# Turning the attention stream over the loop's boundary, own task orders outside the loop, and two PSUM banks kept for the rotary tiles

## The chip, the core and the metric

The kernel runs on one core of one Trainium2 chip. The metric is the device time of one execution in microseconds; the time before is the median of three executions. One execution was also taken by the hardware profiler, and every row shown below is from it.

## The reference

The input is 16 sequences of 512 tokens with 128 features. Each sequence goes through a parameter-free layer norm, and the normed sequence feeds two independent branches, whose results are added to the input:

```python
# branch 1: causal attention, 16 heads of 64
qkv = x @ W_qkv + b_qkv                       # 128 -> 3072
scores = einsum(Q, K) / 8 + causal mask (-10000)
vals = softmax(scores) @ V
branch1 = vals @ W_out + b_out                # 1024 -> 128

# branch 2: two layers of a local transformer, 8 heads of 64, window 64
h = shift_token(x); q, k, v = split(h @ wqkv)     # 128 -> 1536
q, k = l2norm(q) * qs, l2norm(k) * ks
q, k = rotary_xpos(q, k)
o = softmax over own and previous window of 64, masked to distance <= 64
x = x + o @ wo
h = layernorm(shift_token(x)); a, g = split(h @ w1 + b1)
x = x + (a * gelu(g)) @ w2 + b2
```

## The kernel before, in words

Everything works on one sequence at a time, as 4 tiles of 128 tokens. The five engines run one program each, and they all go through the same list of 167 named tasks, `SCHEDULE`; each engine does its own share of each task, in list order. Semaphores link them. A task's name is its kind, the layer where there are two, and the tile or head pair: `("a_max", 3)`, `("f_qk", 1, 2)`.

Attention (`a_...`) takes its 16 heads as 8 pairs. For a pair, PE makes Q and K (`a_proj`, three fp32r products each, since the weights and x are split in a high and a low part), every second pair also V (`a_v`), then scores in bf16 for the row maximum (`a_max`: six PSUM banks, read by VectorE, DVE, at L875), transposes the negated maxima (`a_neg`), makes the transposed fp32 scores with the maxima and the masks added in (`a_st`: six banks, read by ScalarE's exponential at L733), multiplies with V (`a_pv`, once a head), transposes the result (`a_ot`), and adds its share of the output projection into a bank of its own (`a_out`). `a_end` takes that bank out.

The local transformer (`f_...`) of a layer has `f_qk` and `f_v` for each of 4 tiles, then `f_qkt` (transposes of the turned q and k), then 4 head pairs with `f_max`, `f_neg`, `f_st`, `f_pv` and `f_ot`, then `f_wo`, and a serial tail: `f_mean`, `f_var`, `f_rep`, `f_gate`, three `f_up`, `f_down`. In `f_qk`, PE fills two banks (q and k); ScalarE squares each, and DVE reads each four times for the rotary products (L930, L932, L933) and sums the squares (L935), which frees the bank. GpSimd takes the power -1/2 (L662) and scales. `f_wo` ends in DVE's residual addition at L948, once in each layer. `out` closes the sequence.

PSUM has 8 banks. Bank 7 is the output accumulator. The other seven are a ring: each use in the list takes the next bank, whatever it is for, and PE waits in `claim` until the last use of that bank has been read. Since PE goes through the list in order, one slow reader holds up all that comes behind.

The order of the list is made when the program is written out, by `by_ready_time`. It merges three streams greedily: layer 0 of the next sequence with the norm, layer 1 of the current sequence with `out`, and the eight pairs of attention of the current sequence with the transposition `xt` of the next one. Each step takes the stream whose head could start first by a table of costs (`STEPS`), with `f_qk` tasks at least 15 and `a_proj` tasks 20 units apart.

So each pass of the hardware loop does attention and layer 1 of sequence i, and norm, `xt` and layer 0 of sequence i + 1. There are 16 passes. Ahead of them, `before_first` does the tasks that `ahead` names (norm, `xt`, layer 0) for the first sequence, with nothing beside them, and raises the semaphores for those left out. Before that, the setup loads all parameters from the SyncE queue, makes the constants on GpSimd, turns the rotary tables with the scales (L818), and splits W_qkv in six pieces through `yT`, one load, one ScalarE copy (L685) and one DVE subtraction (L824) at a time. The norm of the first sequence comes behind the last subtraction. In the code these are at L559 to L569 (SyncE), L683 to L686 (ScalarE), L813 to L829 (DVE), L1004 to L1007 and L1249 to L1254 (TensorE, PE).

Of the kernel before, what the change touches and what calls it, by code (L numbers as in the profile page):

```python
# [15 lines left out]
P = 128  # L16
# [36 lines left out]
RING = 7  # L53

# [53 lines left out]
ROTARY, PAIR = 15.0, 20.0
# [14 lines left out]
def needs(task):  # L123

    kind, at = task[0], task[1:]
    if kind in ("a_max", "a_st"):
        return [(("a_neg", *at), 9) if kind == "a_st" else (("a_proj", *at), 1)]
# [28 lines left out]
def by_ready_time(streams):  # L156


    free = {"pe": 0.0, "act": 0.0, "dve": 0.0, "pool": 0.0}
    slots, used = [0.0] * RING, 0  # L160
    done, out, n = {}, [], [0] * len(streams)
    rotated = -ROTARY

    def ready(task):
        at = max([done[t][min(k, len(done[t]) - 1)] for t, k in needs(task)], default=0.0)
        if task[0] == "a_proj":
            at = max(at, PAIR * task[1])
        if task[0] == "f_qk":
            at = max(at, rotated + ROTARY)
        for k in range(min(BANKS.get(task[0], 0), 4)):  # L170
            at = max(at, slots[(used + k) % RING])
        return at

    while any(k < len(part) for k, part in zip(n, streams)):
        heads = [(max(ready(part[k]), free["pe"]), side) for side, (k, part) in enumerate(zip(n, streams))
                 if k < len(part) and all(t in done for t, _ in needs(part[k]))]
# [3 lines left out]
        rotated = start if task[0] == "f_qk" else rotated  # L180
# [5 lines left out]
        for k, (engine, us, lead) in enumerate(steps):  # L186
# [3 lines left out]
            if k + 1 == reads:  # L190
                count = BANKS[task[0]]
                for b in range(count):
                    slots[(used + b) % RING] = begun + us * (b + 1) / count
        used += BANKS.get(task[0], 0)
# [4 lines left out]

SCHEDULE = by_ready_time([[("norm",)] + heavy_tasks(0) + tail_tasks(0),  # L200
                          heavy_tasks(1) + tail_tasks(1) + [("out",)],
                          attention_tasks() + [("xt",)]])


def ahead(task):

    return task[0] in ("norm", "xt", "f_first") or (task[0][:2] == "f_" and len(task) > 1 and task[1] == 0)
# [8 lines left out]
assert in_order(("norm",), ("f_first",), ("xt",)) and in_order(("a_proj", PAIRS - 1), ("xt",))  # L216
assert in_order(("a_v", PAIRS // 2 - 1, 1), ("xt",)) and in_order(("a_end",), ("out",))


def earlier(task, which):  # L220


    at = SCHEDULE.index(task)
    for k in range(at - 1, at - 1 - len(SCHEDULE), -1):
        if which(SCHEDULE[k]):
            return SCHEDULE[k], k < 0
    raise ValueError(task)


class Signal:  # L230
# [1055 lines left out]
```

## Time and profile before

| | us |
|---|---|
| three timed executions | 3816.88, 3819.74, 3820.7 |
| median | 3819.74 |
| profiled execution | 3820.81 |
| its span, first to last instruction | 3819.0 |
| PE busy | 3265.4 |
| DVE busy | 2102.0 |
| ScalarE (ACT) busy | 1694.3 |
| GpSimd (POOL) busy | 985.5 |

The busy times are unions of the instructions' durations on an engine. The granted clock, PEclk, is the share of full speed that PE was given, on average over a stretch. "Idle before" is time in which an engine had nothing running, with the instruction that released it. L12 is line 12 of the kernel file.

### The profile page before, as it was taken

The page shows a single profiled execution, that of the slowest core. Times are in us where ns is not written, and L with a number is a line of the kernel's source. Part 1 is how long each engine was busy: PE and PEld are TensorE (multiplying, and loading weights), DVE is VectorE, ACT ScalarE, POOL GpSimd, SP SyncE. Part 2 cuts the span into 40 slices and gives each one's busy share as a digit, 9 for nine tenths or more (in the row PEclk, how much of TensorE's full clock was granted, in tenths as well). Part 3 has the DMA queues.
Part 4 walks back from the last instruction along what each step waited for, and adds up shares of the span by engine and source line. Part 5 has one row for each costly group of instructions (what it writes and reads, how often), then busy time and mean ns, then how long its engine had stood idle before and what let it go on. Part 6 is the DMA issues. An engine that isn't in the chain of part 4 may idle for free.

```text
span 3819.0 us, 95524 instructions
## 1 busy us (share of the span) xinstructions
PE 3265.4 (86%) x35044; PEld 2173.1 (57%) x35044; DVE 2102.0 (55%) x7233; ACT 1694.3 (44%) x3181; POOL 985.5 (26%) x753
## 2 busy tenths in 40 slices
PE   1689898897989889898898989889898988979898
PEld 0356565564656556465565656556565655646565
DVE  2265464646556465564646556464655646465464
ACT  1245354544535445453444535444453535445353
POOL 2132230413224041331303223040322304132140
PEclk9799999999999999999999999999999999999999
DMA  3000000000000000000000000000000000000000
GB/s 79 1 7 2 10 2 10 2 2 10 2 10 2 5 7 2 10 2 10 2 2 10 2 10 2 10 2 2 10 2 10 2 11 2 2 7 2 7 2 4
DMA packets 42468, 26.45 MB, mean 7 GB/s; under 512 B 13107, under 2 KB 40669, under 8 KB 41949
## 3 DMA queue, kind: packets, MB, share of 16 engines
q1 hardware_dynamic: 41948, 19.56, 1.8%
q8 instruction: 323, 5.29, 0.6%
q14 instruction: 197, 1.61, 0.1%
HBM read 14.96 MB, written 4.19 MB: 5 GB/s over the span
## 4 chain that ended last, share of the span: by engine, by line
issue 41%; PE 32%; DVE 16%; ACT 6%; POOL 3%; SPq 1%; DMA 0%; DVEq 0%; ACTq 0%; POOLq 0%; PEldq 0%
PE bank L1103 4%; PE bank L1147 4%; DVE ss L935 3%; PE bank L1190 3%; DVE scratch L930 3%; PE bank L1021 2%; PE bank L1133 2%; DVE scratch L932 2%; PE bank L1205 2%; DVE scratch L933 2%; ACT scratch L767 2%; DVE scratch L943 2%; ACT probs L733 2%; PE bank L1125 2%; PE bank L1175 1%
## 5 line engine op out<-in xcount | busy, mean ns | idle before, releaser
L662 POOL TENSOR_TENSOR rnorm<-ssc,minus_half 128x8 f32<-128x8 f32 x264 | 484.4, 1835 | 991.5 <-DVE ssc L937 988.9
L875 DVE CUSTOM_DVE_ANT_0 bank<-bank,future 128x128 f32<-128x128 f32 (+3 forms) x1024 | 467.3, 529 | 142.1 <-PE bank L1065 140.1
L890 DVE CUSTOM_DVE_ANT_0 bank<-bank,band 128x192 f32<-128x192 f32 x1056 | 341.5, 397 | 281.2 <-PE bank L1084 275.7
L1103 PE MATMUL bank<-Qa,Ka 64*128 64x512 f32 (+3 forms) x2048 | 391.1, 464 | 50.2 <-DVE ss L935 36.1
L733 ACT ACTIVATE probs<-bank 128x512 f32<-128x512 f32 (+1 forms) x768 | 347.0, 530 | 195.8 <-PE bank L1112 195.6
L1147 PEld LDWEIGHTS bank<-Va,probs 128*64 128x64 f32 x10240 | 336.6, 143 | 116.9 <-issue 106.8
L767 ACT ACTIVATE scratch<-bank 128x512 f32<-128x512 f32 x264 | 158.7, 601 | 509.9 <-DVE ss L935 286.3
L1147 PE MATMUL bank<-Va,probs 128*64 128x65 f32 x10240 | 373.1, 230 | 0.7
L651 POOL TENSOR_TENSOR lrstd<-lvar,minus_half 128x4 f32<-128x4 f32 x33 | 33.4, 1012 | 1303.2 <-DVE lvar L953 1303.2
L741 ACT ACTIVATE lprobs<-bank 128x384 f32<-128x384 f32 x528 | 226.8, 491 | 205.1 <-PE bank L1135 202.0
L1190 PE MATMUL bank<-Lqkv,resid 128*128 128x512 f32 x528 | 283.3, 662 | 32.4 <-ACT resid L756 23.4
L930 DVE TENSOR_TENSOR scratch<-bank,rope_t 128x512 f32<-128x512 f32 x264 | 182.6, 692 | 190.3 <-ACT scratch L767 183.9
L1159 PE MATMUL bank<-Vf,lprobs 128*64 128x65 f32 x2112 | 236.9, 227 | 27.1 <-DVE ss L935 16.3
L1133 PE MATMUL bank<-Qf,Kf 64*128 64x192 f32 (+1 forms) x2112 | 241.1, 326 | 0.0
L1159 PEld LDWEIGHTS bank<-Vf,lprobs 128*64 128x64 f32 x2112 | 185.7, 138 | 71.2 <-issue 50.3
L1160 PE MATMUL bank<-Vf,lprobs 128*64 128x65 f32 x2112 | 221.1, 240 | 0.0
L1133 PEld LDWEIGHTS bank<-Qf,Kf 64*128 64x128 f32 x2112 | 182.9, 195 | 34.7
L1103 PEld LDWEIGHTS bank<-Qa,Ka 64*128 64x128 f32 x2048 | 157.8, 187 | 78.0 <-DVE ss L935 46.3
L690 ACT ACTIVATE Qf<-bank 128x512 f32<-128x512 f32 x264 | 160.4, 608 | 85.3 <-PE bank L1021 83.0
L1163 PE MATMUL bank<-Vf,lprobs 128*64 128x65 f32 x1584 | 198.1, 223 | 0.0
L1125 PE MATMUL bank<-outside,row_of 64*128 64x384 bf16 x1056 | 136.3, 336 | 70.1 <-ACT negfT L725 40.1
L690 ACT ACTIVATE Qa<-bank,bqkv 128x512 f32<-128x512 f32 x128 | 89.1, 696 | 239.3 <-PE bank L1016 239.3
(150 smaller groups left out, 7112.1 us busy)
## 6 DMA issues: line engine op xcount, KB each, us to landing
x_res<-in_L_attn_x SPq DMA_DIRECT2D x16, 256.0 KB, 2.9
x_rows<-in_L_attn_x SPq DMA_DIRECT2D x16, 256.0 KB, 3.1
out<-yT SPq DMA_DIRECT2D x16, 256.0 KB, 2.7
Lqkv<-in_L_ffn_wqkv SPq DMA_DIRECT2D x2, 768.0 KB
yT<-in_L_attn_W_qkv SPq DMA_DIRECT2D x6, 256.0 KB, 2.7
rope_t<-in_rope SPq DMA_DIRECT2D x8, 128.0 KB
Lw<-in_L_ffn_w SPq DMA_DIRECT2D x2, 341.0 KB
Lwo<-in_L_ffn_wo SPq DMA_DIRECT2D x2, 256.0 KB
```

The lines of the kernel that those rows point to most:

```text
L662: g.tensor_tensor(rnorm[s][:, :], ssc[s][:, :], minus_half[:, :], ALU.pow).then_inc(rnorm_ready.sem, 1)
L690: psum.raise_read(a.activation(dst, src, func, **kw), task, mark)
L733: psum.raise_read(a.activation(probs[j][:, at:at + n], psum.bank(task, (u, j))[:, 0:n], ACT.Exp, scale=float(HEAD) ** -0.5), task, (u, j))
L767: a.activation(squares, psum.bank(task, c)[:, :], ACT.Square).then_inc(squares_ready.sem, 1)
L875: ins = v.tensor_tensor_reduce(psum.bank(task, (u, j))[:, at:at + n], psum.bank(task, (u, j))[:, at:at + n], future[:, SEQ - n:SEQ], 1.0, ...
L890: ins = v.tensor_tensor_reduce(psum.bank(task, (u, j))[:, k * BAND:(k + 1) * BAND], psum.bank(task, (u, j))[:, k * BAND:(k + 1) * BAND], b ...
L930: v.tensor_tensor(heads(turn_a), src, table(0, 0, HEAD), ALU.mult)
L1103: mm(bank[j][:, at:end], Ka[p % 2][HALF[j], tile(k)], Qa[p % 2][HALF[j], queries], start=True, stop=False)
L1133: mm(bank[j][:, at:at + n], Kf[l][HALF[j], p, tile(t)], Qf[l][HALF[j], p, queries], start=False, stop=False)
L1147: ins = mm(bank[part, t * (HEAD + 1):(t + 1) * (HEAD + 1)], probs[j][:, at + part.start:at + part.stop], Va[p // 2 % 2][:, k, 2 * (p % 2) ...
L1159: mm(bank[HALF[0], to], lprobs[j][:, t, HALF[0]], Vf[l][:, t, 2 * p + j, :], start=True, stop=(t == 0))
L1190: psum.raise_filled(mm(bank[:, :], resid[l][:, tile(t)], Lqkv[l][:, c * INNER:(c + 1) * INNER], start=True, stop=True), task, m)
```

## The change

1. The attention stream is turned by four pairs. `A_BEGUN` is the rounds of pairs up to the middle, `A_REST` the others and `a_end`. A pass now does, in the third stream, `A_REST` of sequence i, then `xt` and `A_BEGUN` of sequence i + 1. `ahead` names `A_BEGUN` too.
2. The loop makes 15 passes. Ahead of it stands the list `FIRST` (norm, layer 0, `xt`, `A_BEGUN` of the first sequence), behind it the list `LAST` (layer 1, `out`, `A_REST` of the last), each ordered by the planner for itself, with 11 and 20 units between `f_qk` and `a_proj`. In the loop they are 15 and 24. `earlier`, `Signal` and `Ring` learn which of the three lists a use is in.
3. The seven banks become two rings: five banks for all uses but `f_qk`, two for `f_qk` alone. `claims` waits for both banks of a pair before the first product.
4. The setup is reordered. SyncE loads x, Lqkv of layer 0, its tables and scales, then W_qkv in two halves into space of layer 1's Q and K tiles, then the rest. GpSimd makes six constants, does its share of the first norm, and makes the rest. The split of W_qkv stands inside `xt` of the first sequence; turned tables of layer 0 stand inside its first `f_qk`, and waits for weights, masks and parameters stand at the first task that needs them.

```diff
 RING = 7
+TURNED, LONG = ("f_qk",), 2
...
+A_BEGUN = [task for r in range(-1, PAIRS // 2) for task in attention_round(r)]
+A_REST = [task for r in range(PAIRS // 2, PAIRS + 1) for task in attention_round(r)] + [("a_end",)]
...
 SCHEDULE = by_ready_time([[("norm",)] + heavy_tasks(0) + tail_tasks(0),
                           heavy_tasks(1) + tail_tasks(1) + [("out",)],
-                          attention_tasks() + [("xt",)]])
+                          A_REST + [("xt",)] + A_BEGUN], 15.0, 24.0)
+FIRST = by_ready_time([[("norm",)] + heavy_tasks(0) + tail_tasks(0), [("xt",)] + A_BEGUN], 11.0, 20.0)
+LAST = by_ready_time([heavy_tasks(1) + tail_tasks(1) + [("out",)], A_REST], 11.0, 20.0)
...
+            names = numbered(marks, run)
+            for size, at, own in ((n - LONG, 0, [name for name in names if name[0][0] not in TURNED]),
+                                  (LONG, n - LONG, [name for name in names if name[0][0] in TURNED])):
+                self.use[id(run)].update({name: (at + k % size, k // size + 1) for k, name in enumerate(own)})
...
+    def claims(self, engine, i, task, marks, after=()):
+        last = self.latest(i, task, after)
+        own = {self.slot(i, task, mark): mark for mark in marks}
+        for slot in [*own, *(slot for slot in last if slot not in own)]:
+            if slot in own:
+                n = self.value(i, task, own[slot], False) - 1
...
+                engine.wait_ge(self.read[slot], n)
...
+            load(x_res[:, :, :], slice(0, 1), x_loaded)
+            sp.dma_start(Lqkv[0][:, :], wqkv[0]).then_inc(whole_qkv[0], 16)
+            turn_tables(0)
+            for k, part in enumerate(staging):
+                sp.dma_start(part, W_qkv[:, k * PIECE:(k + 1) * PIECE]).then_inc(staged[k], 16)
...
+            make_early()
+            steps(-1, FIRST[:1])
+            make_rest()
+            steps(-1, FIRST[1:])
...
                     if kind == "xt":
+                        if isinstance(i, int):
+                            for k in range(WPIECES):
+                                act.wait_ge(staged[k // 3], 16)
+                                a.activation(Wqkv[0][:, k * SEQ:(k + 1) * SEQ], staging[k // 3][:, k % 3 * SEQ:(k % 3 + 1) * SEQ],
+                                             ACT.Copy).then_inc(split_hi, 1)
...
-            with pe.Fori(0, BATCH) as i:
+            steps(-1, FIRST)
...
+            with pe.Fori(0, BATCH - 1) as i:
                 steps(i, SCHEDULE)
+            steps(BATCH - 1, LAST)
```

## Rows read from the trace of the kernel before

**Rows 1.** The page's first section: busy time, share, instructions of each engine.

```profile
PE 3265.4 (86%) x35044; PEld 2173.1 (57%) x35044; DVE 2102.0 (55%) x7233; ACT 1694.3 (44%) x3181; POOL 985.5 (26%) x753
```

**Rows 2.** Stretches: setup, layer 0 alone, loop; length, busy time by engine, PEclk.

```profile
core 0: us, PE busy (x) PEld busy (x) DVE busy (x) ACT busy (x) POOL busy (x), PEclk, DMA share, GB/s
0.00:65.10 65.10, 0.00 (x0) 0.00 (x0) 6.93 (x14) 5.06 (x7) 13.03 (x43) 1.00 0.44 111
65.10:198.90 133.80, 82.30 (x484) 46.29 (x484) 46.16 (x147) 30.09 (x54) 29.67 (x22) 0.77 0.01 3
198.90:3816.80 3617.90, 3183.12 (x34560) 2126.82 (x34560) 2048.88 (x7072) 1659.13 (x3120) 942.83 (x688) 0.97 0.02 5
```

**Rows 3.** Timeline of SyncE's queue: start, length, the first and last store.

```profile
424.55 0.41 SPq L584 DMA_DIRECT2D out<-yT  x1
...
3816.31 0.39 SPq L584 DMA_DIRECT2D out<-yT  x1
```

**Rows 4.** Stretches of one pass of the loop: head, middle, end.

```profile
2013.50:2040.50 27.00, 19.69 (x104) 11.70 (x104) 16.62 (x51) 13.54 (x24) 10.44 (x8) 0.86 0.10 30
2040.50:2220.50 180.00, 165.63 (x2011) 114.00 (x2012) 104.82 (x383) 85.69 (x165) 47.49 (x35) 0.99 0.01 2
2220.50:2238.50 18.00, 12.68 (x48) 6.44 (x47) 6.61 (x10) 4.44 (x6) 1.01 (x1) 1.00 0.01 3
```

**Rows 5.** PE's waits in 14 passes: total us, times, longest.

```profile
PE bank L1065 <- DVE ss L935: 38.9, 14, 2.9
...
PE bank L1103 <- DVE ss L935: 31.5, 28, 1.5
PE bank L1014 <- issue: 28.0, 14, 2.4
PE bank L1125 <- DVE ss L935: 24.1, 14, 1.7
...
PE bank L1159 <- DVE ss L935: 14.3, 14, 1.0
```

**Rows 6.** Groups by line: `f_wo`'s residual addition, once a layer.

```profile
L948 DVE TENSOR_TENSOR resid<-bank,resid 64x512 f32<-64x512 f32 x33 | 22.5, 683 | 139.2 <-PE bank L1205 139.2
```

**Rows 7.** Timeline of the setup: start, length, engine, what, idle before.

```profile
11.02 3.36 SPq L522 DMA_DIRECT2D rope_t<-in_rope  x4
...
36.12 24.70 SPq L565 DMA_DIRECT2D yT<-in_L_attn_W_qkv  x6
...
63.37 0.63 ACT L685 ACTIVATE Wqkv_hi<-yT 128x512 fp32r<-128x512 f32 x1 [3.75 <-DMA yT<-in_L_attn_W_qkv]
64.15 0.69 DVE L824 TENSOR_TENSOR Wqkv_lo<-yT,Wqkv_hi 128x512 fp32r<-128x512 f32 x1 [3.68 <-ACT Wqkv_hi L685]
...
72.09 3.75 PE L1190 MATMUL bank<-Lqkv,resid 128*128 128x512 f32 x4 [1.38 <-ACT resid L756]
```

**Rows 8.** Stretch of the setup in which the DMA moved most.

```profile
25.00:30.00 5.00, 0.00 (x0) 0.00 (x0) 2.77 (x8) 0.00 (x0) 0.00 (x0) 1.00 1.05 334
```

**Rows 9.** Timeline: `f_wo` and the end of layer 0 alone; `f_wo` in a pass.

```profile
165.06 5.37 PE L1205 MATMUL bank<-Qf,Lwo 128*128 128x512 f32 x8 [1.14 <-ACT Qf L690]
...
195.83 0.76 DVE L987 SCALAR_TENSOR_TENSOR resid<-bank,b2s,resid 64x512 f32<-64x512 f32 x1
...
2207.06 3.70 PE L1205 MATMUL bank<-Qf,Lwo 128*128 128x512 f32 x8 [0.53 <-ACT Qf L690]
```

**Rows 10.** Timeline of a pass's head: rotary tile, then the maxima behind it.

```profile
2032.99 1.98 PE L1190 MATMUL bank<-Lqkv,resid 128*128 128x512 f32 x4
...
2035.57 0.69 DVE L930 TENSOR_TENSOR scratch<-bank,rope_t 128x512 f32<-128x512 f32 x1 [4.03 <-ACT scratch L767]
...
2040.45 0.93 PE L1065 MATMUL bank<-Ka,Qa 64*128 64x384 bf16 x4 [2.78 <-DVE ss L935]
2041.13 0.28 DVE L875 CUSTOM_DVE_ANT_0 bank<-bank,future 128x128 f32<-128x128 f32 x1
...
2042.37 0.59 DVE L875 CUSTOM_DVE_ANT_0 bank<-bank,future 128x384 f32<-128x384 f32 x1
```

**Rows 11.** Timeline: PE's first product of the next pass.

```profile
2239.68 0.49 PE L1014 MATMUL bank<-xT_hi,Wqkv_hi 128*128 128x512 f32 x1 [2.27 <-issue]
```

More of the change, by code:

```diff
@@ L153, in needs, with by_ready_time, here @@
         "out": lambda: [("f_down", DEPTH - 1), ("a_end",)]}.get(kind, lambda: [])()]
-def by_ready_time(streams):
+def by_ready_time(streams, rotary, pair):
+    present = [task for part in streams for task in part]
+    def here(task):
+        return [(t, k) for t, k in needs(task) if t in present and not (t in A_BEGUN and task in A_REST)]
     free = {"pe": 0.0, "act": 0.0, "dve": 0.0, "pool": 0.0}
-    slots, used = [0.0] * RING, 0
+    rings = {False: [0.0] * (RING - LONG), True: [0.0] * LONG}
+    used = {False: 0, True: 0}
     done, out, n = {}, [], [0] * len(streams)
-    rotated = -ROTARY
+    apart = {"f_qk": (rotary, -rotary), "a_proj": (pair, -pair)}
     def ready(task):
[L165 to L169, printed above, removed]
+        at = max([done[t][min(k, len(done[t]) - 1)] for t, k in here(task)], default=0.0)
+        at = max(at, sum(apart.get(task[0], (0.0, 0.0))))
+        slots, at_slot = rings[task[0] in TURNED], used[task[0] in TURNED]
         for k in range(min(BANKS.get(task[0], 0), 4)):
-            at = max(at, slots[(used + k) % RING])
+            at = max(at, slots[(at_slot + k) % len(slots)])
         return at
@@ L175, in by_ready_time @@
         heads = [(max(ready(part[k]), free["pe"]), side) for side, (k, part) in enumerate(zip(n, streams))
-                 if k < len(part) and all(t in done for t, _ in needs(part[k]))]
+                 if k < len(part) and all(t in done for t, _ in here(part[k]))]
         start, side = min(heads)
@@ L215, with earlier, before_it, numbered @@
 assert in_order(("norm",), ("f_first",), ("f_qk", 1, 0), ("f_wo", 0), ("f_wo", 1), ("f_down", 0), ("f_mean", 1), ("out",))
[L216 to L226, printed above, removed]
+assert in_order(("norm",), ("f_first",), ("xt",), ("a_proj", 0)) and in_order(("a_proj", PAIRS - 1), ("xt",))
+assert in_order(("a_v", PAIRS // 2 - 1, 1), ("xt",)) and in_order(("a_end",), ("out",)) and in_order(("a_end",), ("a_out", 0))
+def earlier(i, task, which):
+    run = run_at(i)
+    for other in reversed(run[:run.index(task)]):
+        if which(other):
+            return other, False
+    for other in reversed(SCHEDULE):
+        if which(other):
+            return other, True
     raise ValueError(task)
+def before_it(i, task, other):
+    return earlier(i, task, lambda t: t == other)[1]
+def numbered(marks, run):
+    return [(task, m) for task in run for m in marks.get(task[0], ())]
 class Signal:
@@ L1121, in steps @@
                         for u in range(2):
[L1122 removed]
+                            bank = psum.claims(pe, i, task, [(u, j) for j in range(2)], after if u == 0 else [])
                             for k in range(2):
```

618 lines of the change are left out of this document (331 added, 287 removed).

## The prediction

> **What bounds the kernel now.** I read the page's busy line first: TensorE (PE) is busy 3265.4 of 3819.0 us, VectorE (DVE) 2102.0 and ScalarE less, so PE is the bound, and 14% of the span is PE idle [rows 1]. Then the busy time by stage, to see where that idle time lies [rows 2]: the setup, 65.1 us, in which PE does nothing; layer 0 of the first sequence alone, 133.8 us with PE busy 82.3; the loop, 3617.9 us, which is 16 passes of 226.1 us (the stores say the same: (3816.31 - 424.55) / 15 = 226.1 [rows 3]). With the last store's landing that is 65.1 + 133.8 + 3617.9 + 2.2 = 3819.0 us, and 3820.8 us for the profiled execution, 1.1 us over the median of the timed runs. All sums below are made against 3820.8.
>
> Inside a pass the view by stretches splits 225 us in three [rows 4]: the first 27 us have PE idle for 7.3 us and a granted clock of 0.86; the middle 180 us have 14.4 us idle at 0.99; the last 18 us have 5.3 us idle. PE's list of waits over 14 passes names the causes [rows 5]: four lines wait for DVE's reduction at L935, which frees a rotary bank, 38.9 + 31.5 + 24.1 + 14.3 = 108.8 us, or 7.8 us a pass, and `a_proj` waits 2.0 us a pass at the loop's branch. So PE's work in a pass is 226.1 - 27.1 = 199 us as it stands.
>
> **The change part by part.**
>
> *One layer pass goes.* L948 runs once in each layer of each sequence, and it ran 33 times, not 32 [rows 6]: the last pass of the loop also did a layer 0 for a sequence that does not exist. Now FIRST + 15 passes + LAST hold exactly 16 passes' work. FIRST and LAST are together one pass's tasks, cut by layer: layer 0 with attention pairs 0 to 3, then layer 1 with pairs 4 to 7. So what is removed is one pass of 226.1 us; what is added is that FIRST is longer than layer 0 alone, and LAST comes on top.
>
> *Setup.* Before, norm waited for six turns of load, split and release of `yT`: the loads are issued from 36.1 to 60.8 us, the last split is at 64.15, and the first projection of the layer starts at 72.1 [rows 7]. Now norm waits for x and six small constants only. SyncE issues x, Lqkv, ten rope and scale loads and the two halves of W_qkv, 14 DMAs; at the 0.84 us that a rope table's issue took [rows 7] 12 us. They carry 256 + 768 + 512 + 96 + 1536 KB = 3.2 MB, at the 334 GB/s of the busiest stretch [rows 8] 9.7 us. The weight split (six ACT copies of 0.63 us, six DVE subtractions of 0.69) sits inside `xt`, which the planner puts close behind `f_first`, so ACT holds the layer's first square until W_qkv is in. So I take the layer's first projection as starting, in effect, at 22 us, the sum of the two, instead of 72. Bounds: 12 us (nothing blocks) and 41 us (the transfers run at a third of that rate). The masks and weights(0), issued later, are wanted only tens of us on.
>
> *FIRST.* Layer 0 alone took from 72.1 to 196.6 us, 124.5 us [rows 7, 9], at a mean clock of 0.77 [rows 2]. Its `f_wo` took 5.37 us there and 3.70 us in the loop [rows 9]: the difference is the clock. At full clock 82.3 us of PE become about 82.3 x 0.77 = 63, so the chain alone would be 105 to 110 us. Half of the attention is (195 - 126) / 2 = 34 us of PE work (195 is derived below, 126 are two layers of 63). It fits into the layer's idle PE time, but PE takes its tasks in one order, and each layer task can find PE or DVE in the middle of an attention task of 1 to 4 us: I add 25 us. FIRST is 133 us, bounds 110 (all hidden) and 165 (34 us of PE and the loss of clock both in full).
>
> *LAST.* The same chain of layer 1, plus `out` and the store, 6 us: 139 us, bounds 116 and 170. Nothing follows, so its whole length counts.
>
> So outside the loop there are 22 + 133 + 139 us, with 2 us of loop entry and 2 us to the landing of the store: 298 us (ends, all at once: 242 and 380; 275 to 325 is likely). Were a pass still 226.1 us, the total would be 298 + 15 x 226.1 = 3690 us. That much asks only for the work to be cut as the code cuts it.
>
> *The turned stream.* Now the end of layer 1 (the serial walk from mean over gate and up to out, PE idle 5.3 of 18 us) has attention pairs 0 to 3 of the next sequence beside it, and the head of a pass, norm and first projection, has pairs 4 and on. Idle time at both ends is 7.3 + 5.3 = 12.6 us [rows 4]; 2.8 of it is a rotary-bank wait [rows 10], counted below, and 2.3 us is the branch: PE stands still from the pass's end until `a_proj` at 2239.68 [rows 11], and that stays. 7.5 us can go. The clock: 27 us at 0.86 are 7.6 us at the half level (1.2 GHz), which PE is busy for about three quarters; full clock gives back roughly half of the busy part, with the bits of the middle stretch 4 us a pass. Hence PE's real work is about 199 - 4 = 195 us. The lowered clock stands behind the idle walk at a pass's end each time, and comes back after it; if the walk is filled, I expect it not to fall.
> The Trainium skill (TensorE: Matmul & The Clock Gate, Part 1) says that the throttled state is the default and activity releases it, and also that for modelling the ramp is under 1% of a kernel's span. The first agrees with the 0.77 of the idle-ridden layer; the second does not with a loop mean of 0.97. By the page's 1% the loop's refund would be at most 36 us, by the rows 15 x 4 = 60 us, so its sum would be 24 us higher.
>
> *Two banks set apart, five for the rest.* The 7.8 us of waits for L935 go: DVE holds the rotary pair for 4.9 us, from L930 at 2035.57 until PE is let go at 2040.45, and the maxima's next bank waited 2.78 us behind it [rows 10]. But all other tasks have five banks where they had seven. `a_max` takes six: its third pair now needs the first pair read. DVE begins at 2041.13 and starts on the third bank at 2042.37, 1.24 us [rows 10]; PE has about 0.4 us of the second pair to do, so 0.8 us are new in each of 8 `a_max`, 6.4 us a pass, with DVE free. `a_st` takes six too, but PE makes them no faster than ACT reads them (2.9 against 3.2 us in the planner's own figures). Bounds: 0 (those stalls hide in waits that would have come anyway), and 16 us (DVE, busy 57% of the time, comes 1.2 us late on average).
>
> *A pass then:* 226.1 - 7.8 - 7.5 - 4 + 6.4 = 213.2 us, PE busy 91% of it. Bounds 206.8 and 222.8.
> The new pair spacing of 24 against 20 moves no work; 8 x 24 = 192 in the planner's own units just spreads the attention over the pass.
>
> *Sum:* 298 + 15 x 213.2 = 3496, plus 1.8 around the span: 3498 us profiled, 3497 us as the median.
>
> **The rivals.**
>
> *A. The five banks eat the gain.* At their upper bound a pass is 222.8 us: 298 + 3342 + 2 = 3642 us. For it: PE wants some 297 bank uses in a pass, one each 0.72 us, so each of five banks must turn in 3.6 us, and one `a_max` keeps DVE 3.9 us by the planner's own figure. Against: the rotary waits were found at only four lines.
> The Trainium skill (Trainium Kernel Development and Optimization, Best Practices) says to mind PSUM pressure, since PE work speeds up and its evacuation does not; here that is this rival.
>
> *B. The ends stay empty.* If the planner's order puts the early pairs before the walk and none in it, 7.5 and 4 us stay: 226.1 - 7.8 + 6.4 = 224.7 us a pass, 3670 us. For it: the planner counts `f_qk` as 0.9 us of PE while its four products take 1.98 us at full clock and 3.75 at half [rows 7, 10], so its clock runs ahead of the chip's. Against: the attention stream is the longest of the three.
>
> *C. All hides.* The five banks cost nothing: 206.8 us a pass, 298 + 3102 + 2 = 3402 us.
>
> *D. Slower.* The third pair of each `a_max` waits for DVE's full rotary block of 4.9 us: 206.8 + 8 x 4.9 = 246.0 us a pass, 3990 us. It decides from (3819.7 - 300 - 15 x 206.8) / 15 / 8 = 3.5 us for each `a_max`. Against: the block stands before 8 of 8 maxima only if the planner pairs them so, and the longest single wait for DVE in the loop is 2.9 us [rows 5].
>
> *E. The cut is not worth what it says:* FIRST and LAST at their long ends with the loop as forecast, 3570 us; it lies in the range.
>
> **How the numbers follow.** Forecast 0.56 (E in it), A 0.20, B 0.08, C 0.12, D 0.04. The range runs from C, 3400, to B, 3670. About 0.2% (8 us) is what can be told from no change. Only D reaches it: faster 0.96, same 0.01, slower 0.03.
>
> **What would show it.** L948 x32 and L1205 x256; the first `f_qk` product at 20 to 25 us; stores 213 us apart; LAST some 139 us from the last branch; granted clock in the loop 0.99 and more, none under 0.9 at a pass's head; no PE wait for L935 in the loop; L1065 waiting for L875 some 0.8 us, 8 times a pass. I am wrong if stores stand more than 223 us apart, if PE waits for DVE at L875 or L890 sum to over 16 us a pass, or if FIRST ends after 190 us.

## The result, and the profile after

The changed kernel takes 3901.23 us (median of 4 runs, 3898.54 to 3903.88), the kernel before 3818.31 us beside it (4 runs). The ratio is 1.0217 with a 95% interval of 1.0200 to 1.0235: slower by 2.2%, where 3497 us and faster were forecast. The profiled execution has a span of 3896.6 us and took 3898.5.

The stages of after come first (columns as in [rows 2]): setup to the first `f_qk` product, FIRST, the 15 passes, LAST.

```profile
0.00:20.28 20.28, 1.94 (x8) 1.60 (x9) 5.85 (x18) 6.15 (x10) 14.37 (x44) 1.00 0.59 162
20.28:144.40 124.12, 107.80 (x1092) 70.61 (x1092) 67.32 (x234) 52.29 (x100) 28.65 (x21) 0.95 0.14 35
144.40:3776.57 3632.17, 3078.18 (x32404) 2024.04 (x32400) 1934.01 (x6635) 1590.73 (x2940) 884.19 (x645) 0.95 0.02 5
3776.57:3896.60 120.03, 98.96 (x1064) 66.10 (x1060) 60.01 (x201) 47.20 (x91) 28.64 (x21) 0.97 0.01 3
```

Outside the loop stand 20.3 + 124.1 + 120.0 = 264.4 us, where 298 were forecast. The whole loss is in the loop, as the stores on SyncE's queue show (answering [rows 3]):

```profile
361.35 0.41 SPq L634 DMA_DIRECT2D out<-yT  x1
...
3754.36 0.39 SPq L634 DMA_DIRECT2D out<-yT  x1
3893.93 0.39 SPq L634 DMA_DIRECT2D out<-yT  x1
```

(3754.36 - 361.35) / 14 = 242.4 us a pass, against 226.1 before and 213.2 forecast. The stretch of those 14 passes in both kernels, before first:

```profile
424.55:3590.15 3165.60, 2785.10 (x30240) 1860.37 (x30240) 1792.09 (x6187) 1451.69 (x2730) 824.96 (x602) 0.97 0.02 5
```

```profile
361.35:3754.36 3393.01, 2875.39 (x30242) 1889.93 (x30240) 1803.59 (x6188) 1484.79 (x2744) 825.24 (x602) 0.95 0.02 5
```

PE executes the same number of products (30242 against 30240) and is busy 205.4 us a pass where it was 198.9. Idle time grew too, from 27.2 to 37.0 us. So 16.2 us were added to a pass, 9.8 of them idle and 6.4 busy. Most of the busy part is the granted clock, which is 0.95 for 0.97 on the mean. In the trace's clock records it stands either at full speed or at half. PE was busy at half speed for 11.2 us of a pass before and for 19.5 us in after; half of that is what the clock cost, 5.6 and 9.7 us. That is 4.1 of the 6.4 us. The other 2.3 us come with five banks in place of seven: without the clock's part the products keep PE busy 193.2 to 193.6 us a pass in every kernel with seven banks, and 194.9 to 196.2 in every one with five (the filler's aside). No run shows why.

PE's waits in 14 passes (answering [rows 5]: line waited at, releaser, us, times, longest):

```profile
PE bank L1143 <- DVE neg L946: 171.3, 112, 5.1
PE bank L1241 <- DVE negf L961: 68.0, 14, 4.9
PE bank L1170 <- DVE negf L961: 47.5, 70, 1.1
PE bank L1091 <- issue: 46.0, 14, 3.5
```

L1143 is the products of `a_max` (L1065 before), L1170 the transposes of the negated maxima, L1241 the products of `f_pv`, L1091 those of `a_proj`, L946 and L961 are DVE's row maxima (L875, L890), and L1008 is the rotary reduction (L935). No wait of PE for L1008 is left, where there were 7.8 us a pass. In its place `a_max` waits 12.2 us a pass and `f_pv` 4.9; the transposes of the band's maxima (L1170) wait 3.4, and the loop's branch 3.3, where it was 2.0 [rows 5]. The 12.2 us are eight waits, and in one pass they are 0.51, 0.74, 5.13, 0.51, 1.90, 1.88, 0.74 and 0.82 us. The longest, from PE's timeline (start, length, what, idle before it):

```profile
2094.96 0.52 PE L1143 MATMUL bank<-Ka,Qa 64*128 64x128 bf16 x6
2100.61 0.61 PE L1143 MATMUL bank<-Ka,Qa 64*128 64x512 bf16 x2 [5.13 <-DVE neg L946]
2101.15 2.07 PE L1259 MATMUL bank<-OaT,Wout 128*128 128x512 f32 x2
2103.15 2.29 PE L1229 MATMUL bank<-Va,probs 128*64 128x65 f32 x40
```

DVE in the same time:

```profile
2094.08 0.69 DVE L1003 TENSOR_TENSOR scratch<-bank,rope_t 128x512 f32<-128x512 f32 x1 [7.55 <-ACT scratch L831]
...
2098.30 0.68 DVE L1008 TENSOR_REDUCE ss<-scratch 128x8 f32<-128x512 f32 x1
2099.01 0.81 DVE L1010 TENSOR_SCALAR ssc<-ss 128x8 f32<-128x8 f32 x1
2099.73 0.28 DVE L946 CUSTOM_DVE_ANT_0 bank<-bank,future 128x128 f32<-128x128 f32 x1
```

PE's list has `f_qk 0.0`, `f_v 0.0`, `a_max 5`. PE writes the first banks of `a_max` within a microsecond, but DVE stood still for 7.55 us until ACT's squares came, then serves the rotary tile from 2094.08, and begins the maxima at 2099.73. On a ring of five the third pair of banks needs the first pair read, so PE stands 5.1 us. That is rival D's mechanism, at one `a_max` of eight instead of at all; the 1.90 us are a second case, `a_max 7` behind `f_qk 0.3`.

The Trainium skill (PSUM — Partial Sum Buffer, Engine vs sequencer instructions) says that ScalarE's, VectorE's and GpSimdE's queues are strict FIFO. The trace agrees: the first four banks of `a_max` lay filled from 2095.5 on, while DVE went on with the rotary tile until 2099.7.

The other long one is `f_max 0.3` behind `f_qk 1.2`. There PE waits at a later task, `f_pv`, whose bank `f_max` still holds (DVE's rotary block, then DVE's first maximum, then PE):

```profile
2187.99 0.69 DVE L1003 TENSOR_TENSOR scratch<-bank,rope_t 128x512 f32<-128x512 f32 x1 [3.28 <-ACT scratch L831]
...
2193.28 0.37 DVE L961 CUSTOM_DVE_ANT_0 bank<-bank,band 128x192 f32<-128x192 f32 x1 [0.29 <-issue]
```

```profile
2194.07 0.37 PE L1241 MATMUL bank<-Vf,lprobs 128*64 128x65 f32 x1 [4.86 <-DVE negf L961]
```

What a stall costs beyond its own length is in the row behind it: 40 products at L1229 took 2.29 us at 2103.15, and 1.39 us at full clock (in x6 below). Cut in 25 slices, the pass from 2056.7 on has seven slices under 0.95, these five among them (the other two are 0.89 and 0.85):

```profile
2076.10:2085.80 9.70, 6.58 (x92) 4.88 (x92) 3.37 (x17) 3.25 (x4) 1.01 (x1) 0.76 0.03 8
2085.80:2095.50 9.70, 8.34 (x58) 4.24 (x54) 2.15 (x7) 5.06 (x10) 0.00 (x0) 0.88 0.18 54
2095.50:2105.20 9.70, 4.59 (x42) 2.68 (x44) 7.76 (x24) 1.08 (x2) 7.05 (x5) 0.65 0.01 2
...
2134.30:2144.00 9.70, 6.32 (x41) 3.21 (x41) 8.91 (x27) 2.63 (x5) 7.96 (x6) 0.76 0.00 0
...
2192.50:2202.20 9.70, 8.13 (x92) 6.24 (x93) 4.31 (x22) 2.92 (x7) 0.00 (x0) 0.82 0.00 0
```

They lie at the loop's branch (2079 to 2082), at the 5.13, at the 1.90 and behind the 4.86. The middle of a pass, 0.99 before [rows 4], now has clock gaps of its own.

### The profile page after: what moved, and what is told of

It is laid out like the page before. It is cut to its first block, busy times and chain, and to the rows that moved or that the text cites. A ratio compares the mean times of both kernels' runs of the same rounds, so it can differ in the third digit from the quotient of the medians.

```text
span 3896.6 us, 93798 instructions
## 1 busy us (share of the span) xinstructions
PE 3286.9 (84%) x34560; PEld 2162.3 (55%) x34560; DVE 2067.2 (53%) x7086; ACT 1696.4 (44%) x3140; POOL 955.9 (25%) x731
## 4 chain that ended last, share of the span: by engine, by line
PE 64%; DVE 17%; issue 11%; ACT 3%; POOL 2%; DVEq 0%; ACTq 0%; POOLq 0%
PE bank L1183 8%; PE bank L1229 8%; PE bank L1215 4%; PE bank L1277 4%; PE bank L1098 3%; PE bank L1294 3%; PE bank L1259 3%; PE bank L1091 3%; DVE ss L1008 3%; PE bank L1207 2%; DVE bank L961 2%; PE bank L1327 2%; PE bank L1317 2%; PE bank L1093 2%; PE bank L1092 2%
## 5 line engine op out<-in xcount | busy, mean ns | idle before, releaser
L716 POOL TENSOR_TENSOR rnorm<-ssc,minus_half 128x8 f32<-128x8 f32 x256 | 469.4, 1834 | 975.8 <-DVE ssc L1010 973.4
L946 DVE CUSTOM_DVE_ANT_0 bank<-bank,future 128x128 f32<-128x128 f32 (+3 forms) x1024 | 469.3, 524 | 270.3 <-PE bank L1143 269.8
L961 DVE CUSTOM_DVE_ANT_0 bank<-bank,band 128x192 f32<-128x192 f32 x1024 | 330.7, 393 | 208.2 <-PE bank L1162 203.9
L1229 PEld LDWEIGHTS bank<-Va,probs 128*64 128x64 f32 x10240 | 347.7, 148 | 138.1 <-issue 110.9
L1183 PE MATMUL bank<-Qa,Ka 64*128 64x512 f32 (+3 forms) x2048 | 408.3, 481 | 6.3 <-issue 6.0
L1229 PE MATMUL bank<-Va,probs 128*64 128x65 f32 x10240 | 384.1, 235 | 3.3 <-DVE negf L961 3.2
L1143 PE MATMUL bank<-Ka,Qa 64*128 64x128 bf16 (+3 forms) x1024 | 139.9, 321 | 228.0 <-DVE neg L946 189.5
L1241 PE MATMUL bank<-Vf,lprobs 128*64 128x65 f32 x2048 | 240.4, 233 | 77.7 <-DVE negf L961 72.9
L787 ACT ACTIVATE negT<-bank 128x512 bf16<-128x512 bf16 x128 | 76.5, 598 | 476.7 <-PE bank L1170 475.7
L1277 PE MATMUL bank<-Lqkv,resid 128*128 128x512 f32 x512 | 257.0, 625 | 30.4 <-ACT resid L820 19.8
L705 POOL TENSOR_TENSOR lrstd<-lvar,minus_half 128x4 f32<-128x4 f32 x32 | 32.4, 1012 | 1012.0 <-DVE lvar L1026 1012.0
L1241 PEld LDWEIGHTS bank<-Vf,lprobs 128*64 128x64 f32 x2048 | 186.9, 142 | 113.3 <-DVE negf L961 79.0
L1215 PE MATMUL bank<-Qf,Kf 64*128 64x192 f32 (+1 forms) x2048 | 224.0, 317 | 0.0
L1143 PEld LDWEIGHTS bank<-Ka,Qa 64*128 64x128 bf16 x1024 | 43.7, 94 | 323.1 <-issue 173.9
L702 POOL TENSOR_TENSOR rstd<-var_eps,minus_half 128x4 f32<-128x4 f32 x16 | 16.1, 1007 | 715.9 <-DVE var_eps L905 715.9
```

Source lines behind the costliest of these rows:

```text
L716: g.tensor_tensor(rnorm[s][:, :], ssc[s][:, :], minus_half[:, :], ALU.pow).then_inc(rnorm_ready.sem, 1)
L946: ins = v.tensor_tensor_reduce(psum.bank(i, task, (u, j))[:, at:at + n], psum.bank(i, task, (u, j))[:, at:at + n], future[:, SEQ - n:SEQ], ...
L961: ins = v.tensor_tensor_reduce(psum.bank(i, task, (u, j))[:, k * BAND:(k + 1) * BAND], psum.bank(i, task, (u, j))[:, k * BAND:(k + 1) * BAND],
L1183: mm(bank[j][:, at:end], Ka[p % 2][HALF[j], tile(k)], Qa[p % 2][HALF[j], queries], start=True, stop=False)
L1215: mm(bank[j][:, at:at + n], Kf[l][HALF[j], p, tile(t)], Qf[l][HALF[j], p, queries], start=False, stop=False)
L1229: ins = mm(bank[part, t * (HEAD + 1):(t + 1) * (HEAD + 1)], probs[j][:, at + part.start:at + part.stop], Va[p // 2 % 2][:, k, 2 * (p % 2) ...
```

## The experiments

All runs are timed against the kernel before in 3 rounds (5 for the filler). Pass and busy time are those of the profiled execution, between the first and the fifteenth store (before: of the stretch shown above); the last column is the part of the busy time that the clock cost, half of what PE was busy at half speed.

| kernel | us | ratio [95%] | pass | PE busy | of it clock |
|---|---|---|---|---|---|
| before | 3818.3 | 1 | 226.1 | 198.9 | 5.6 |
| after | 3901.2 | 1.0217 [1.0200, 1.0235] | 242.4 | 205.4 | 9.7 |
| x1_after_order_one_ring | 3810.7 | 0.9982 [0.9968, 0.9996] | 236.3 | 203.5 | 10.1 |
| x2_one_ring | 3689.8 | 0.9673 [0.9650, 0.9695] | 228.9 | 200.0 | 6.4 |
| x3_other_order_split | 3932.6 | 1.0295 [1.0258, 1.0331] | 245.5 | 211.8 | 16.9 |
| x4_unturned_one_ring | 3681.3 | 0.9661 [0.9633, 0.9690] | 225.6 | 198.8 | 5.4 |
| x5_unturned_split | 3851.6 | 1.0094 [1.0070, 1.0119] | 236.5 | 204.2 | 8.1 |
| x6_filler | 3858.2 | 1.0104 [1.0087, 1.0120] | 238.9 | 207.3 | 5.6 |
| x7_maxima_ahead | 3765.4 | 0.9860 [0.9836, 0.9883] | 232.8 | 200.4 | 4.1 |
| x8_walk_filled | 3595.9 | 0.9411 [0.9391, 0.9430] | 222.6 | 197.7 | 4.3 |
| x9_walk_and_moves | 3686.9 | 0.9662 [0.9646, 0.9678] | 228.7 | 201.3 | 8.1 |
| x10_x9_split | 3829.0 | 1.0045 [1.0028, 1.0062] | 237.7 | 205.7 | 9.7 |
| x11_ring_of_five | 4047.1 | 1.0595 [1.0564, 1.0627] | 251.3 | 211.4 | 15.6 |
| x12_x7_one_ring | 3731.5 | 0.9774 [0.9746, 0.9802] | 230.4 | 199.5 | 6.2 |

**Ring against order.** The split does two things: it changes the banks, and it changes the picture by which the planner orders the lists (`by_ready_time` models the banks). x1 keeps the lists of after and takes one ring of seven; x2 has one ring in the planner too; x3 runs x2's lists on split rings.

```diff
 # x2: on the line of the rings, before the lists are made
-TURNED, LONG = ("f_qk",), 2
+TURNED, LONG = (), 0
 # x1: the same line behind the lists, so that only the ring changes; x3: x2, and behind the lists
+TURNED, LONG = ("f_qk",), 2
```

> The changed kernel with its three task lists word for word, but on one ring of seven banks. A pass is 242.4 us in the changed kernel. Theory R (the five-bank ring is what costs: PE stands 12.2 us a pass at the third pair of a_max, and the clock falls behind those stalls): the stalls at L1143 and most of the lowered clock go, the rotary waits for L1008 come back at 8 us, a pass is about 222 us, the total 3590 us. Rival O (the order is what costs: 28 layer tasks in a row without attention, then 17 attention tasks in a row behind out): a pass stays within 238 to 243 us, the total 3830 to 3900 us.

> The changed kernel with the two banks given back, and the lists planned anew for one ring of seven (the longest row of layer tasks without attention is then 13, and 3 attention tasks stand behind out). Theory R: as the one-ring kernel with the changed kernel's lists, 220 to 224 us a pass, 3590 us. Rival O: order and ring are both repaired, 212 us a pass, 3450 us, and at least 15 us a pass under the kernel with only the ring undone.

> The lists that are planned for one ring of seven, run on the split rings of five and two. Theory R: the third pair of a_max still waits for the first, 12 us a pass and the clock behind it, 238 to 243 us a pass, 3850 us. Rival O: the order is repaired, so 215 to 222 us a pass, 3530 us.

The split costs 242.4 - 236.3 = 6.1 us a pass on the list made for it, and 245.5 - 228.9 = 16.6 us on the other. The list made for it costs 236.3 - 228.9 = 7.3 us on one ring (on the split rings it is the better one, 242.4 against 245.5). So both were at fault. No theory had the sizes: x1 lies under rival O's 238 to 243 us and far over theory R's 222, x2 over both forecasts, x3 over both. With one ring and its own list the change is faster than before, by 3.3%. Of x3's 16.6 us, 4.8 are idle time and 11.8 are busy time for the same products, 10.5 of them clock.

x1 also shows what the 5.13 us would be with seven banks. This is the same place, `f_v 0.0` and `a_max 5`, in a pass of x1:

```profile
2047.53 0.52 PE L1144 MATMUL bank<-Ka,Qa 64*128 64x128 bf16 x6
2051.67 0.61 PE L1144 MATMUL bank<-Ka,Qa 64*128 64x512 bf16 x2 [3.63 <-DVE ss L1009]
2052.21 2.07 PE L1260 MATMUL bank<-OaT,Wout 128*128 128x512 f32 x2
```

On this list `f_qk`, `f_v` and `a_max` want nine banks in a row, so with a ring of seven too the third pair must wait, for the rotary pair to be read: 3.63 us here and 2.22 at `a_max 7`, 5.8 us a pass, with the same slow products behind both (2.07 us). On this list the split therefore takes away 10.1 us a pass of waits for the rotary reduction and brings 13.6 of waits for maxima. It adds nothing to what the clock costs, 9.7 against 10.1 us.

Waits of x3 and then of x2, in 14 passes:

```profile
PE bank L1144 <- DVE neg L947: 79.2, 98, 2.4
PE bank L1099 <- POOL kn L727: 48.9, 14, 3.5
PE bank L1092 <- issue: 46.7, 14, 3.6
PE bank L1092 <- DVE Of L981: 30.2, 14, 2.2
```

```profile
PE bank L1098 <- POOL kn L726: 50.0, 14, 3.6
PE bank L1091 <- issue: 45.6, 14, 3.9
PE bank L1170 <- DVE negf L961: 38.4, 42, 1.3
PE bank L1143 <- DVE ss L1008: 37.4, 14, 2.7
```

The split takes away the wait for the rotary reduction (37.4 us) and puts 79.2 and 30.2 us of waits for DVE in its place.

**The cut without the turn.** x4 has FIRST, LAST and the new setup, but the loop does the attention of its own sequence as before, in the planner's list with its old spacings of 15 and 20, on one ring. x5 runs the same lists on split rings.

```diff
-TURNED, LONG = ("f_qk",), 2
+TURNED, LONG = (), 0
...
-A_BEGUN = [task for r in range(-1, PAIRS // 2) for task in attention_round(r)]
-A_REST = [task for r in range(PAIRS // 2, PAIRS + 1) for task in attention_round(r)] + [("a_end",)]
+A_BEGUN = []
+A_REST = [task for r in range(-1, PAIRS + 1) for task in attention_round(r)] + [("a_end",)]
...
-                          A_REST + [("xt",)] + A_BEGUN], 15.0, 24.0)
+                          A_REST + [("xt",)] + A_BEGUN], 15.0, 20.0)
 # x5: x4, and behind the lists
+TURNED, LONG = ("f_qk",), 2
```

> Only the cut of the work and the new setup: the loop's list is exactly that of the kernel before, on one ring of seven; FIRST is layer 0 alone, LAST is layer 1 and all eight pairs. Both theories: a pass is 226.1 us as before, layer 0 alone 125 us from 20 us on, LAST some 195 us; 20 + 125 + 2 + 15 x 226.1 + 195 + 2 = 3736 us. If a pass is not within 1 us of 226.1, something in the new waits costs by itself.

> The kernel with only the cut and the setup (225.5 us a pass, 3681 us), its lists unchanged, on the split rings of five and two: the split alone. Theory D (DVE serves in list order, so a rotary block of 4.9 us still stands before the maxima queued behind it, and with five banks PE has used up its ring before DVE gets there): the rotary waits of 7.5 us a pass go, waits for the maxima and a lower clock of 14 to 20 us a pass come, 233 to 240 us a pass, 3800 to 3900 us. Rival S (the split only hurts in a turned order): 220 to 226 us a pass, 3600 to 3690 us.

x4's pass is that of before (225.6, forecast for it 226.1). Its time is 3681 us, 55 less than was expected of it: layer 0 alone takes 105.0 us (from 20.82 to 125.86) where 125 were expected, and LAST 165 (from 3509.1 to 3674.5) where 195 were. The cut and the setup alone gave 3.4%. The split costs 10.9 us here, as theory D has it. And turning the stream, by the planner's list, lengthened the pass by 3.4 us (x4 to x2), where 11.5 less was forecast. The slices of x2 show why. This is its bare walk from `f_down` to `f_gate` at the end of a pass, with the slices beside it:

```profile
2155.00:2164.50 9.50, 8.96 (x98) 4.92 (x96) 4.84 (x12) 1.10 (x3) 0.00 (x0) 1.00 0.00 0
2164.50:2174.00 9.50, 5.76 (x21) 3.39 (x22) 1.06 (x3) 3.28 (x5) 1.01 (x1) 0.72 0.00 0
2174.00:2183.50 9.50, 9.50 (x57) 5.30 (x57) 2.25 (x3) 6.03 (x9) 0.00 (x0) 0.92 0.01 2
```

PE has 21 products in 9.5 us: the planner put `f_down 0, f_mean 1, f_var 1, f_rep 1, f_gate 1` in a row with attention only before and behind. In after it is another clump, 28 layer tasks without attention in the middle of the pass and 17 attention tasks behind `out`.

**The maxima ahead of the rotary tile (x7), and the clock kept by filler (x6).**

```diff
 # x7, behind the lists of after
+moved(SCHEDULE, ("a_max", 5), ("f_qk", 0, 0))
+moved(SCHEDULE, ("a_max", 7), ("f_qk", 0, 3))
+moved(SCHEDULE, ("f_max", 0, 3), ("f_qk", 1, 2))
 # x6, ahead of the third pair of a_max 5 (18 times) and a_max 7 (8 times)
+for _ in range(FILL.get((p, u), 0)):
+    mm(out_acc[:, :], zeros[:, :], future[:, :], start=False, stop=False)
```

> The changed kernel with products of a zero tile put in just ahead of PE's two stalls at the third pair of a_max: 18 for pair 5 (the stall of 5.13 us) and 8 for pair 7 (1.90 us), accumulated as zeros into the output bank; they add work and no result. Theory C (the clock falls because PE stood idle, and the work behind the stall then runs at 1.2 GHz): the stalls are filled, the output projection behind pair 5 takes 1.0 us in place of 2.07, a_pv 1.4 in place of 2.29, and a pass is 2 to 5 us shorter though PE does more, 3820 to 3870 us. Rival: the low clock is not tied to the stall, the filler is at best free, 242 to 244 us a pass, 3890 to 3920 us.

> The changed kernel with three tasks moved in the loop's list: a_max 5, a_max 7 and f_max 0 3 now stand ahead of the f_qk that stood ahead of them (f_qk 0 0, 0 3 and 1 2), so that DVE reads the maxima before its rotary block. Theory D: the waits of 5.1, 1.9 and 4.9 us go and the clock behind them comes back, 227 to 233 us a pass, 3670 to 3760 us. Rival R (five banks are too few whatever the order): the waits move to the next maxima, 239 to 243 us a pass, 3850 to 3900 us.

Three tasks moved, no bank and no product changed: the pass falls by 9.5 us, to 232.8, as theory D has it (the time, 3765 us, is 5 over its range). Waits of x7 in 14 passes, at the lines that were 171.3 and 47.5 in after:

```profile
PE bank L1156 <- DVE neg L959: 77.3, 98, 1.9
PE bank L1183 <- DVE negf L974: 47.0, 70, 1.1
```

94 of the 171.3 us and all of the 68.0 at `f_pv` are gone, 11.6 us a pass; most of it came back at other lines, above all L1272, L1111 and L1220 (119 us in 14 passes). Idle time fell by 4.5 us and busy time by 5.0, since the clock gave back 5.6.

x6 leaves the stall and fills it with products of zeros. Its timeline at the place of the 5.13 us:

```profile
2072.66 3.83 PE L1142 MATMUL bank<-future,zeros 128*128 128x512 bf16 x17 [0.16 <-issue]
2077.64 0.40 PE L1147 MATMUL bank<-Ka,Qa 64*128 64x512 bf16 x2 [1.14 <-DVE neg L948]
2077.97 1.12 PE L1263 MATMUL bank<-OaT,Wout 128*128 128x512 f32 x2
2079.02 1.39 PE L1233 MATMUL bank<-Va,probs 128*64 128x65 f32 x40
```

The wait for DVE ends where it ended, but the products behind it run at full clock: 1.12 and 1.39 us where after had 2.07 and 2.29. The pass is 3.4 us shorter with more work in it: PE is idle 5.3 us less, has 6.0 us more to do, and gets 4.2 back from the clock. These 4.2 us are the clock's share of two stalls, apart from the stalls themselves.

**Does the split cost only where DVE has a rotary tile in front?** x12 is x7 on one ring.

> x7's lists (those of after, with the maxima a_max 5, a_max 7 and f_max 0.3 ahead of the rotary tasks) on one ring of seven. Theory D (five banks cost only where DVE serves a rotary block ahead of the maxima, and x7 has mended the three worst places): the split is nearly free on these lists, the pass stays within 2.5 us of x7's 232.8, time 3730 to 3770 us. Theory R (five banks are short at the maxima whatever stands ahead of them): one ring saves 6 to 11 us a pass as on the other lists, 222 to 227 us, time 3600 to 3680 us.

230.4 against 232.8: on these lists the split costs 2.4 us a pass, where on the lists of after it cost 6.1. So 3.7 of the 6.1 us were those three places. The three moves also gave one ring 5.9 us (236.3 to 230.4), since there the maxima waited for a bank of the rotary pair itself (81.8 us in 14 passes in x1, none in x12). So the three places were also most of the 7.3 us by which that list is worse than x2's on one ring.

**The walk filled by hand (x8).** x2 with the last 23 tasks of the loop's list set by hand, attention between any two of the walk except the first two `f_up`:

```diff
+WALK = [("f_down", 0), ("a_pv", 2, 0), ("f_mean", 1), ("a_neg", 3), ("a_pv", 2, 1), ("f_var", 1), ("a_proj", 4), ("f_rep", 1),
+        ("a_v", 2, 0), ("f_gate", 1), ("a_st", 3), ("f_up", 1, 0), ("f_up", 1, 1), ("a_ot", 2), ("f_up", 1, 2), ("a_max", 4),
+        ("f_down", 1), ("a_v", 2, 1), ("a_out", 2), ("a_pv", 3, 0), ("out",), ("a_neg", 4), ("a_pv", 3, 1)]
+SCHEDULE = [task for task in SCHEDULE if task not in WALK] + WALK
```

> The turned kernel on one ring of seven (228.9 us a pass, 3690 us), with the last 23 tasks of its list put in turn: one attention task between any two of the walk from f_down 0 over f_mean, f_var, f_rep, f_gate, f_up and f_down of layer 1 to out. If turning failed because the planner left that walk bare (PE busy 5.8 of 9.5 us at a clock of 0.72 there), a pass is 5 to 8 us shorter, 221 to 224 us, 3570 to 3615 us, under the unturned one. Rival: the walk's own length ends the pass, or the idle time moves to the head, 227 to 229 us, 3665 to 3690 us.

The pass falls from 228.9 to 222.6 us, 3.0 under the unturned one, and the kernel is the fastest of all, 0.9411 of before. Slices over the same place of a pass of x8:

```profile
2110.00:2119.50 9.50, 9.50 (x106) 5.85 (x105) 4.66 (x10) 1.57 (x3) 0.00 (x0) 1.00 0.00 0
2119.50:2129.00 9.50, 8.62 (x57) 5.12 (x56) 0.91 (x2) 6.63 (x9) 1.01 (x1) 1.00 0.01 2
2129.00:2138.50 9.50, 9.33 (x58) 4.62 (x54) 6.93 (x21) 4.21 (x9) 0.00 (x0) 1.00 0.00 1
```

In no slice is PE idle for more than 0.9 us or the clock under 1.00, where x2 had PE busy 5.76 of 9.50 us, at 0.72. Of the 6.3 us, 4.0 are idle time and 2.3 busy, nearly all of it clock.

**Two more moves on x8 (x9), and that list split (x10).** Two waits stood out in x8: 3.57 us for POOL's `kn` at L1102, and 2.67 us for L1012 (the rotary reduction) in front of `a_max 7`.

```diff
+moved(SCHEDULE, ("a_max", 7), ("f_qk", 0, 3))
+moved(SCHEDULE, ("f_qkt", 0, 0), ("a_st", 5))
```

> One ring of seven banks, the turned stream, the layer-1 walk filled with attention as in x8, and two tasks moved in the loop's list: the maxima of attention pair 7 ahead of the rotary task f_qk 0.3 (in x8 PE waited 2.67 us at L1147 behind DVE's rotary block there), and the transposes f_qkt 0.0 from ahead of f_v 0.1 to ahead of a_st 5 (in x8 PE waited 3.57 us there for POOL's kn). Theory D (a stall is one task too early in PE's list, and goes whole when the task is moved): pass 222.6 - 2.7 - 3.6 = 216.3 us, or 217 with some clock not regained, 3595.9 - 15 x 5.9 = about 3507 to 3525 us. Rival W (the wait only wanders to the next instruction, since DVE and POOL are late anyway): under 1.5 us a pass, 3575 to 3596 us.

> The same lists as x9, on split rings of five and two banks. So far the split cost 6.1, 10.9 and 16.6 us a pass on three lists, and the list with fewest waits of DVE behind rotary blocks was not among them. Theory D (the split is dear only where maxima stand behind a rotary block in DVE's list, and one such place in layer 0 is mended here): 2 to 6 us a pass over x9, 3540 to 3610 us. Theory R (five banks are too few for the maxima of a pair as such: PE must wait for the third pair's banks nearly every time): 8 to 17 us a pass over x9, 3630 to 3780 us, with PE's waits at L1147 for DVE at L950 of 60 us or more in 14 passes.

x9 failed on both theories: the pass grew by 6.1 us, 2.5 of them idle and 3.6 busy, which is clock. The two waits went, and PE's timeline has longer ones a few tasks on (`f_qkt 0.0`, `a_st 5`, then `f_qkt 0.3` twice):

```profile
1993.50 0.63 PE L1112 MATMUL bank<-ident,kn 128*128 128x128 f32 x4 [1.97 <-DVE ss L1022]
1996.19 2.08 PE L1197 MATMUL bank<-Qa,Ka 64*128 64x512 f32 x4 [2.07 <-DVE ss L1022]
...
2029.21 0.97 PE L1112 MATMUL bank<-ident,qn 128*128 128x128 f32 x4 [2.47 <-POOL qn L740]
2033.52 1.11 PE L1112 MATMUL bank<-ident,kn 128*128 128x128 f32 x4 [3.33 <-POOL kn L740]
```

With `a_max 7` in front, DVE reaches the rotary tile of `f_qk 0.3` later, POOL's `qn` and `kn` come later, and `f_qkt 0.3` waits 5.8 us for them, where x8 had 2.67 us at `a_max 7` and 1.45 at `a_neg 7`. The other move took 3.57 us away and brought 1.97 and 2.07 for the next rotary tile. The 11.1 us from 2033.52 on have a granted clock of 0.72. One of the three moves that together paid in x7 cost here. x10 says that the split costs 9.0 us on this list; by x7 and x12 I had expected 2 to 6, and theory R's 8 to 17 holds, though not its mark: the waits at `a_max` for maxima sum to 59.0 us in 14 passes, just under its 60.

**The number of banks or their being apart?** x11 is x2's lists on one ring of five, two banks lying idle (`RING = 5` behind the lists).

> x2's lists on one ring of five banks for all uses, the rotary tiles among them; two banks lie idle. Against x2 (seven, 228.9 us a pass) and x3 (five and two apart, 245.5). Theory R (what costs is that only five banks serve the maxima; the two set apart give something back): as slow as x3 or slower, 246 to 265 us a pass, 3940 to 4230 us. Rival P (what costs is the setting apart, since each ring turns unevenly, and not the number): faster than x3, 233 to 243 us a pass, 3750 to 3900 us.

251.3 us a pass: as theory R says. Against x3 (245.5) the two banks set apart give back 5.8 us; against x2 the two banks missing cost 22.4. So it is the number of banks for the rest that is dear, not that the rings are apart.

## Why the prediction was wrong

*Outside the loop* the mechanism was right and the sizes were too high: setup 20.3 us (forecast 22), FIRST 124.1 (133 + 2), LAST 120.0 (139 + 2), 264.4 for 298, which is under the 275 that was called likely. In x4 the layer alone takes 105.0 us, so the four pairs beside it in FIRST cost 19 us, not 25; the clock is 0.95 and 0.97 instead of 0.77. (Rival E's 3570 us is a slip: its own terms add to 3561.) One pass's work less is there as said; POOL's L705, once a layer, from the page's groups (columns as in [rows 6]):

```profile
L705 POOL TENSOR_TENSOR lrstd<-lvar,minus_half 128x4 f32<-128x4 f32 x32 | 32.4, 1012 | 1012.0 <-DVE lvar L1026 1012.0
```

x4's 3681 us stand near my intermediate sum of 3690, but by luck: x4 is cut elsewhere, with all eight pairs behind the loop. With the cut as made, 264.4 us outside and 226.1 a pass would be 3658 us.

*The failed steps are in the pass*, 242.1 us for 213.2 (242.4 between the stores), times 15 about 434 us; less the 34 us gained outside, 400 of the miss of 404 us. Most of the rest is the median, which lies 2.7 us over the profiled execution.

- "The 7.8 us of waits for L935 go": right, none is left.
- "0.8 us are new in each of 8 `a_max`, 6.4 us a pass, with DVE free": eight waits did come, and five were 0.5 to 0.8 us. Three were 1.88, 1.90 and 5.13, so 12.2 us, and `f_max`, which I had not costed on five banks, brought 4.9 us more at `f_pv`. The fault is "with DVE free". I had priced DVE's two tasks one at a time, though [rows 10] show that DVE holds a rotary pair for 4.9 us, and before it stood still for 4.03 us waiting for ACT. I gave that mechanism (D) 0.04, at 8 of 8 or nothing. Three places were enough, `a_max 5`, `a_max 7` and `f_max 0.3`: x7, which moves only these, takes 9.5 us off the pass. The split is not their only cause. With seven banks the same list stands 3.63 and 2.22 us at the first two (x1) and loses 5.9 us a pass by the three together (x12).
- "Full clock gives back 4 us": the reverse came. By the clock records the loss was 5.6 us a pass before, not 4, and it is 9.7 in after. On this list it grew with the order and not with the split: 5.4 in x4, 6.4 in x2, 10.1 in x1, which has after's list on seven banks. I priced stalls by their length alone. x6 shows the surcharge: 4.2 us of clock a pass for two stalls.
- "Idle time at both ends, 7.5 us can go": it did not. With one ring rival B's condition came, the planner left the walk bare (x2), and the pass grew by 3.4 us over x4's; in after the planner's clumps are elsewhere, and the pass's head still has 0.76 and 0.88 of the clock. x8 shows that the gain exists if the walk is filled, -6.3 us against x2 but only -3.0 against x4, a quarter of the 11.5 forecast. The branch wait, which "stays" at 2.0 us a pass, is 3.3 in after and 3.3 in x2.
- Not in the prediction at all: the split changes the planner's lists. That cost 7.3 us a pass on seven banks (x1 against x2), more than the split itself on that list, and 5.9 of it are the three places.

Added up, from x4: turn +3.4, list +7.3, split +6.1 make the 16.8 us by which after's pass is over x4's. The shares depend on the order of the steps: by way of x3 the split is +16.6 and the list -3.1.

The Trainium skill (TensorE: Matmul & The Clock Gate, Part 1) puts the ramp under 1% of a typical kernel's span. It says so of the products with which a kernel starts, so the prediction's comparison with the loop's refund did not fit. Here the clock falls in every pass: it cost 5.6 of 226.1 us before, 2.5%, and 9.7 of 242.4 in after, 4.0%.

The marks held where they stood for single steps (first `f_qk` product at 20.28 us, no wait for the rotary reduction, eight waits at `a_max`) and two of the three that were to prove me wrong did (stores 242 us apart; waits for maxima 171.3 + 68.0 + 47.5 us in 14 passes, 20.5 us a pass, over 16); FIRST ended well before 190 us, at 144.4. "0.99 and more in the loop, none under 0.9 at a pass's head" failed too: 0.95, with 0.76 and 0.88 at the head.

*What stays open.* The split costs 2.4, 6.1, 9.0, 10.9 and 16.6 us on five lists. Of the 6.1 I can name the places for 3.7. For x2's list, 10.5 of the 16.6 us are clock behind stalls of at most 3.6 us, and I have not shown which of them sets it off. x9's idle time can be told apart by move, as above, but not its 3.6 us of clock. Why the same products keep PE busy some 2 us longer with five banks, apart from the clock, is not shown either.

## What to carry to other kernels

Before a ring of buffers is divided, look for every burst that fills more of them than the smaller ring holds (and for those that already fill more than the whole ring), and ask what its reader has in front of it in its own queue at that moment, with its waits for third engines: here 4.9 us of rotary work, not the 1.2 us that the first buffer takes. Price a stall of the tensor engine with the clock behind it: over half its length again for the two stalls that x6 filled (4.2 us for 5.13 + 1.90), and more than the idle time saved for the three places that x7 mended (5.6 us of clock, 4.5 idle). If a planner models the resource that is changed, run its old list on the new resource and its new list on the old one: two runs that tell a change of order from a change of hardware use, and a list set by hand can show whether the gain is there at all.

## What the runs showed of the hardware

- The same products kept PE busy 197.7 us a pass in x8 and 211.8 in x3 (mean granted clocks of 0.98 and 0.92); 12.7 of the 14.1 us between them are clock. The clock stood at one of two levels, 1.2 and 2.4 GHz. A slice in which PE was busy most of the time could have a low mean too, as this one of x3 with 0.67:

```profile
2164.23:2174.47 10.24, 8.53 (x100) 5.91 (x102) 5.71 (x22) 1.66 (x3) 4.80 (x4) 0.67 0.01 2
```
- Two stalls filled with products of zeros (x6): behind the longer one the clock stayed at its higher level (1.39 us for the 40 products that took 2.29), and 26 useless products a pass made the kernel 1.1% faster (3901 to 3858 us, each timed beside before).
- PE's idle time at the loop's branch depends on what stands around it: 2.0 us a pass before, 3.3 us in after and x2, with a branch of the same kind; why is not shown.
